# Moving the pair-maximum steps to other key-tile slots, and collecting the value products of long rows in groups of three, three and two

## The chip, the cores and the metric

One program runs on one core of a Trainium2 chip. The metric is the device time of one execution in microseconds (us): the median of three runs.

## The reference

Eight images of 1024 tokens and 256 channels pass through one block: a layer norm with a shift and a scale from a small modulation network, attention with 16 heads, a gated residual, a second layer norm, a mixture of 16 experts of which each token and head takes two, and a second gated residual. The part that the change touches is the attention:

```python
q = jnp.concatenate([q_content, q_rope], axis=-1)      # 16 + 32 columns a head
k = jnp.concatenate([k_content, k_rope], axis=-1)
scores = jnp.einsum('bhqd,bhkd->bhqk', q, k) * scale
scores = jnp.where(causal[None, None], scores, -jnp.inf)
attn = jax.nn.softmax(scores, axis=-1)
out = jnp.einsum('bhqk,bhkd->bhqd', attn, v)           # v: 16 columns a head
```

## The kernel before

The images follow one another. Each has an attention phase (about 161 us) and an expert phase (about 193 us) in which the next image's projections, and the first steps of its attention, are woven into the expert work. TensorE (PE in the profile), VectorE (DVE), ScalarE (ACT), GpSimd (POOL) and SyncE (SP, which only issues DMAs) each run one written order of instructions, and semaphores tie them.

**Slots.** The 16 heads make four groups `g`, the 1024 queries two halves `c`. A row is one (g, c), and `SEQ` orders the eight rows: (0,0), (1,0), (0,1), (2,0), (3,0), (1,1), (2,1), (3,1). A row of c = 0 has four key tiles of 128 keys, a row of c = 1 has eight, because the mask is causal. `MAIN` lists all 48 (g, c, key tile): they are the slots 0 to 47. Rows of eight key tiles take the slots 8 to 15, 24 to 31, 32 to 39 and 40 to 47. On the diagonal the moving side shrinks: the last four key tiles of a row have 512, 384, 256 and 128 query columns.

In a slot TensorE runs `scores` twice (L1279; one call is two heads of the group, four matmul instructions into two PSUM banks). ScalarE takes the exponential of each call from PSUM into a slot of the buffer `pt` (L1393), and GpSimd zeroes what the mask cuts (L1508). A call of `scores` may start when the exponential of the call before the last has freed its two banks. `values` (L1305) multiplies the exponentials of one key tile with the values: eight instructions for four heads. After every second slot the values of the last two key tiles are multiplied, so they stand at the end of the slots 2, 4, 6 and so on, and the last two in the first expert step. `pt` holds `PTS` = 6 calls, three key tiles, so the exponential of slot N waits for the values of slot N - 3.

**Pairs of maxima.** The exponentials need a bound of each query's scores. It comes from a second, cheaper multiplication in another number format: an item "pair" (L428) is two PSUM banks of such scores, and VectorE reduces each bank to a maximum (L573 where the mask cuts, L576 where it does not). An item stands in one of three parts of a slot: between the two calls of `scores`, behind the second, or in front of what follows. In the images after the first, 47 pairs are placed in the attention phase, and `PLACES` says where: (slot, part), part 0 being between and part 1 behind. In the first image other places are used (`per_slot`), two or three pairs in many slots.

**The ring.** Pairs and all other small items of the attention phase share a ring of three PSUM banks (6, 7, 5) in the order in which they are written down. A pair takes two of them. So a pair that follows another pair directly waits until VectorE has read the first bank of that one; if an item of one bank stands between the two, it waits for both banks. TensorE runs in order, so the calls of `scores` and the values behind a waiting pair wait with it. VectorE reads the items in the same order. When the last pair of a row is read, a `row` item (L500) turns the maxima, and SyncE moves them into the operand of the scores (L780, four DMAs) before the row begins.

Other items of the phase: `rope` (L477, L479), `sums` (L505: the row's outputs, turned), `tr` (L510), `o` (L518: the output projection, followed on VectorE by statistics), `xn` (L649 on VectorE: the second layer norm, four instructions), `tr2`, `tm`, `lg` and the choice of experts. At slot 22 VectorE multiplies three sets of weights by gates (L1474, L1476, L1478).

`L.va` holds the values: 32 columns a head, of which 16 are values, one is 1.0 (for the sum of the softmax) and 15 are 0.0. It lies in the region `front`; `pt` and, later, the expert buffers lie in the region `rest`.

Of the kernel before, what the change touches and what calls it, by code (L numbers as in the profile page):

```python
# [21 lines left out]
B, T, C = 8, 1024, 256  # L22
# [8 lines left out]
NP = NH // 2  # L31
MROW = QD
VW = 32
SCALE = float(QD) ** -0.5
NEG = -1e38
PTS = 6
FH, FD, NE, FI = 8, 32, 16, 128
XS = 3 * FD + 2
EPS_RMS, EPS_LN = 1e-6, 1e-5
# [145 lines left out]
        all_images(nc, L, Opening(nc, L))  # L185


FRONT_WORDS = 15248
HEADS_WORDS = 4096
WIDE_WORDS = 12288  # L190
REST_WORDS = 10496


class Regions:
# [25 lines left out]

    def place(self, L):
        self.begin("front")
        L.va = self.take("front", NT, NH, VW)
        base = self.at["front"]
        L.ht = self.take("front", CH, T)
        L.qct = self.take("front", T)
        L.ck = self.take("front", 2, T)
        L.rc = self.take("front", 2, T)
        L.rt = self.take("front", 3, 2, HALF)
        L.mx0 = self.take("front", NG, 4 * HG)  # L230
        L.mx1 = self.take("front", NG, 4 * HG, 2)
# [12 lines left out]
        gt0 = self.take("front", HALF)  # L244

        self.begin("heads")
        self.begin("wide")
        qk = [self.take("heads", 2, T) for _ in range(2)] + [self.take("wide", 2, T) for _ in range(6)]
        L.q2, L.k2 = qk[0::2], qk[1::2]
        self.begin("wide")  # L250
        L.x2 = self.take("wide", 2, FH, HALF)[0:XS].bitcast(F32R)
        L.gb = self.take("wide", 4, 2, HALF)

        self.begin("rest")
        L.wfg = self.take("rest", CH, C)
        L.bog = self.take("rest", C)
        own = self.at["rest"]
        L.wog = self.take("rest", CH, C)
        shared = self.at["rest"]
        L.pt = self.take("rest", PTS, 2, HALF)  # L260
        L.ot = self.take("rest", 2, HALF)
        self.begin("rest", REST_WORDS - 2 * HALF)
        L.junk_a = [self.take("rest", HALF) for _ in range(2)]

        self.begin("rest", shared)
        L.hm = self.take("rest", 4, T)
        L.ct = self.take("rest", CH, T)
        L.gy = self.take("rest", 3, HALF)
        L.kvt = self.take("rest", HALF)
        self.take("rest", HALF)  # L270
        part = self.take("rest", HALF)
        self.begin("rest", own)
        L.junk_b = [part, self.take("rest", HALF)]
        L.kvsq = L.junk_b[0]
        L.gt = [gt0, L.junk_b[0]]
        L.xn = L.ao
        L.cq = L.ao[:, :, :].rearrange("p t c -> p (t c)").rearrange("p (a t) -> p a t", a=2)
# [134 lines left out]
def item_matmuls(pe, L, R, item):  # L412
# [98 lines left out]
    elif kind == "o":  # L511
        c, n = item[1:]
        R.wait(pe, L, ("tr", c, CH - 1))
        if c == 0:
            pe.wait_ge(S["d0_w"], 5)
        for t in range(2):
            for k in range(CH):
                mm = pe.matmul(out[:, t * C:(t + 1) * C], L.at[:, k, (2 * n + t) * P:(2 * n + t + 1) * P], L.wog[:, k, :],  # L518
# [230 lines left out]
def front_ones(g, L):  # L749

    g.memset(L.va[:, :, :, HD:HD + 1], 1.0).then_inc(L.S["f_one"], 1)
    g.memset(L.va[:, :, :, HD + 1:VW], 0.0).then_inc(L.S["f_one"], 1)


def input_ones(sp, L, c):
# [141 lines left out]
class Opening:  # L897
# [4 lines left out]
    def __init__(self, nc, e):  # L902
# [5 lines left out]
        self.ct = e.lay.view("rest", 4352, CH, B)  # L908
        self.cs = e.lay.view("rest", 4368, CH, B)
        self.m01 = e.lay.view("rest", 5376, 2 * C)[0:B]  # L910
        self.m25 = e.lay.view("rest", 8448, 4, C)[0:B]
        self.g1 = e.lay.view("rest", 0, 2, C)[0:B]
        self.g2 = e.lay.view("rest", 768, 2, C)[0:B]
        self.wmod = e.wmod.rearrange("(k p) n -> p k n", p=P)
# [188 lines left out]

AHEAD = 2
EARLY = 3
PLACES = [(1, 0), (2, 0), (3, 0), (5, 0), (7, 0)]
PLACES += [(s, part) for s in range(9, 37) for part in range(2 - s % 2)]


def attend_slots(img):  # L1110
# [3 lines left out]
    if img:  # L1114
        slots[1][1].extend([("out", 2), ("out", 3)])
        places = PLACES
        pairs = [("pair", 1, *p) for p in PAIRS[1][AHEAD:AHEAD + 5]]
        pairs += [("pair", g, *p) for g in (2, 3) for p in PAIRS[0]]
        pairs += [("pair", 1, *p) for p in PAIRS[1][AHEAD + 5:]]
        pairs += [("pair", g, *p) for g in (2, 3) for p in PAIRS[1]]  # L1120
    else:
        per_slot = [(0, 2), (1, 2), (2, 3), (3, 2), (4, 3), (5, 3), (8, 2), (9, 1), (10, 2), (11, 2), (12, 3), (13, 1), (14, 2), (15, 1),
# [98 lines left out]
    return SEQ.index((g, c)) if j == 4 * c + 3 else None  # L1221


def unit(u):

    return u // (4 * NE), u // (2 * NE) % 2, u // 2 % NE, u % 2


def all_images(nc, L, O):
# [18 lines left out]
    with nc.Block() as block:  # L1248
        @block.tensor
        def _(pe):  # L1250
# [33 lines left out]
            def values(img, N):  # L1284
                g, c, j = MAIN[N]
                f = first_query(c, j)
                pe.wait_ge(S["c_exp"], 2 * (N + 1))
                if diag_upto[N]:
                    pe.wait_ge(S["c_sel"], diag_upto[N])
                if N == 0 and img:  # L1290

                    pe.wait_ge(S["e_gy"], NQ - 1)
                    RE[img - 1].wait(pe, L, ("v", 1))
                elif N == 0:

                    pe.wait_ge(S["f_one"], 2)
                    O.R.wait(pe, L, ("v", 1))
                    name, count = O.R.last(PVB)
                    pe.wait_ge(S[name], count)
                if j == 0 and SEQ.index((g, c)):  # L1300

                    pe.wait_ge(S["c_o"], SEQ.index((g, c)))
                for h in range(HG):
                    u = 2 * N + h // 2
                    mm = pe.matmul(bank(PVB)[h * VW:(h + 1) * VW, f:HALF], L.va[:, j, HG * g + h, :],  # L1305
                                   L.pt[:, u % PTS, h % 2, f:HALF], start=(j == 0), stop=(j == 4 * c + 3))
                mm.then_inc(S["c_pv"], 1)

# [36 lines left out]
            for img in range(B):  # L1345
                for s, (between, behind, front) in enumerate(aslots[img]):
# [10 lines left out]
                        outer(img - 1, NQ - 1)  # L1357
                    for item in behind + front:
                        item_matmuls(pe, L, RA[img], item)
                    if s and s % 2 == 0:  # L1360
                        values(img, s - 2)
                        values(img, s - 1)
                for q in range(NQ):
                    inner(2 * q)
                    inner(2 * q + 1)
                    if q == 0:
                        values(img, NM - 2)
                        values(img, NM - 1)
                    if q:
                        outer(img, q - 1)  # L1370
                    for item in eslots[img][q]:
# [6 lines left out]
        def _(act):  # L1378
            def weights(img, N, pr):
# [1 line left out]
                f = first_query(c, j)  # L1381
                u = 2 * N + pr
                act.wait_ge(S["c_s"], u + 1)
                if N >= 3:

                    act.wait_ge(S["c_pv"], N - 2)
                elif N == 2 and img:

                    act.wait_ge(S["c_rp"], RA[img].start["out", 3] + 1)
# [13 lines left out]
            def gelu(u):  # L1403
# [3 lines left out]
                    act.wait_ge(S["e_l2"], (u - HM) // 2 + 1)  # L1407
                else:

                    act.wait_ge(S["c_pv"], NM - 2 + u // 2)  # L1410
                nc.scalar.activation(L.hm[:, u % HM, :], bank(2 * (u % 2), 2), ACT.Gelu).then_inc(S["e_gelu"], 1)  # L1411

            O.scalar(act)
# [17 lines left out]
        def _(v):  # L1431
# [29 lines left out]
            for img in range(B):  # L1461
                for s, (between, behind, front) in enumerate(aslots[img]):
# [6 lines left out]
                    if s == 22:  # L1469
# [3 lines left out]
                        for k in range(CH):  # L1473
                            v.tensor_tensor(L.wog[:, k, :], L.wos[:, k, :], L.gate[:, 0, :],  # L1474
                                            ALU.mult).then_inc(S["d0_w"], 1)
                            v.tensor_tensor(L.wfg[:, k, :], L.wfs[:, k, :], L.gate[:, 1, :],  # L1476
                                            ALU.mult).then_inc(S["d0_w"], 1)
                        v.tensor_tensor(L.bog[:, :], L.bor[:, :], L.gate[:, 1, :], ALU.mult).then_inc(S["d0_w"], 1)  # L1478
# [214 lines left out]
```

## Time and profile before

| | us |
|---|---|
| Median of three runs | 2917.65 (2917.25 to 2918.07) |
| The profiled execution | 2920.5 |
| Its span, first to last instruction | 2918.1 |
| PE busy | 2816.6 (97%) |
| DVE busy | 1863.0 (64%) |
| ACT busy | 1808.5 (62%) |
| POOL busy | 1246.2 (43%) |
| PE L1279 (scores), two groups | 486.3 and 168.0 |
| PE L1305 (values) | 290.2 |
| PE L428 (pairs), two groups | 269.9 and 75.5 |

Starts and durations are in microseconds from the span's start. In a row of the timeline the two numbers are the start and the length of a run of like instructions, and a bracket tells for how long the engine stood idle before and what released it. Matmul instructions overlap, so a cost is best read from start to start.

### The profile page before, as it was taken

The page shows a single profiled execution, that of the slowest core. Times are in us where ns is not written, and L with a number is a line of the kernel's source. Part 1 is how long each engine was busy: PE and PEld are TensorE (multiplying, and loading weights), DVE is VectorE, ACT ScalarE, POOL GpSimd, SP SyncE. Part 2 cuts the span into 40 slices and gives each one's busy share as a digit, 9 for nine tenths or more (in the row PEclk, how much of TensorE's full clock was granted, in tenths as well). Part 3 has the DMA queues.
Part 4 walks back from the last instruction along what each step waited for, and adds up shares of the span by engine and source line. Part 5 has one row for each costly group of instructions (what it writes and reads, how often), then busy time and mean ns, then how long its engine had stood idle before and what let it go on. Part 6 is the DMA issues. An engine that isn't in the chain of part 4 may idle for free.

```text
span 2918.1 us, 50109 instructions
## 1 busy us (share of the span) xinstructions
PE 2816.6 (97%) x16476; PEld 1241.9 (43%) x16476; DVE 1863.0 (64%) x4638; ACT 1808.5 (62%) x2148; POOL 1246.2 (43%) x1325
## 2 busy tenths in 40 slices
PE   7899999999999999999999999999999999999999
PEld 3344444444444443444444444444444444444433
DVE  5775666756666666666667666675756657667553
ACT  2346675566755677457675576655666566665687
POOL 4312645136451364414654146531565215561254
PEclk9899999999999999999999999999999999999999
DMA  6203453044430444304432055311453124530343
GB/s 156 57 5 99 118 130 73 1 108 122 120 71 8 119 118 107 71 21 121 122 97 61 23 134 130 87 47 46 121 133 89 32 71 119 124 88 20 77 127 94
DMA packets 176972, 252.96 MB, mean 87 GB/s; under 512 B 50509, under 2 KB 83293, under 8 KB 176621
## 3 DMA queue, kind: packets, MB, share of 16 engines
q1 hardware_dynamic: 176100, 248.44, 34.3%
q8 instruction: 136, 2.23, 0.3%
q10 hardware_dynamic: 620, 1.34, 0.2%
q14 instruction: 116, 0.95, 0.1%
HBM read 159.13 MB, written 12.63 MB: 59 GB/s over the span
## 4 chain that ended last, share of the span: by engine, by line
PE 86%; DVE 7%; issue 3%; ACT 2%; POOL 1%; SPq 1%; DMA 1%; ACTq 0%; DVEq 0%; POOLq 0%
PE ps L1279 17%; PE ps L1321 17%; PE ps L1339 16%; PE ps L1305 9%; PE ps L428 7%; PE ps L477 4%; PE ps L479 2%; PE ps L518 2%; PE ps L548 2%; DVE rest L573 1%; PE ps L529 1%; PE ps L505 1%; PE ps L536 1%; PE ps L463 1%; PE ps L487 1%
## 5 line engine op out<-in xcount | busy, mean ns | idle before, releaser
L1411 ACT ACTIVATE rest<-ps 128x1024 f32<-128x1024 f32 x1024 | 993.8, 1024 | 341.1 <-PE ps L1321 340.9
L1393 ACT ACTIVATE rest<-ps 128x1024 f32<-128x1024 f32 (+3 forms) x768 | 610.2, 809 | 537.4 <-PE ps L1279 511.6
L1518 POOL TENSOR_TENSOR rest<-rest 128x512 f32<-128x512 f32 x478 | 632.0, 1322 | 560.7 <-DVE rest L1448 548.1
L1448 DVE SCALAR_TENSOR_TENSOR rest<-ps,b2c,wide 128x512 f32<-128x512 f32 x512 | 384.0, 750 | 489.8 <-PE ps L1339 451.7
L1321 PE MATMUL ps<-wide,w1s 98*128 98x512 f32 x2048 | 655.1, 437 | 11.5 <-ACT rest L1411 8.7
L1339 PE MATMUL ps<-rest,w2s 128*32 128x512 f32 x4096 | 546.1, 605 | 0.6 <-ACT rest L1411 0.6
L1508 POOL TENSOR_SCALAR_AFFINE_SELECT rest<-rest 128x256 f32<-128x256 f32 x512 | 206.4, 411 | 772.3 <-ACT rest L1393 770.3
L573 DVE CUSTOM_DVE_ANT_0 rest<-ps,maskd 128x512 f32<-128x512 f32 (+3 forms) x1024 | 444.8, 487 | 118.8 <-PE ps L428 114.0
L1279 PE MATMUL ps<-wide 49*128 49x512 f32 (+3 forms) x2304 | 486.3, 511 | 10.2 <-ACT rest L1393 4.2
L1321 PEld LDWEIGHTS ps<-wide,w1s 98*128 98x128 f32 x2048 | 340.8, 188 | 301.0 <-ACT rest L1411 189.0
L576 DVE TENSOR_REDUCE front<-ps 128x1 f32<-128x512 f32 x512 | 329.0, 684 | 92.9 <-PE ps L428 88.7
L428 PE MATMUL ps<-wide 48*128 48x512 f32 (+3 forms) x1152 | 269.9, 500 | 37.8 <-DVE front L573 20.7
L1305 PE MATMUL ps<-rest,front 128*32 128x512 f32 (+3 forms) x3072 | 290.2, 496 | 0.0
L1279 PEld LDWEIGHTS ps<-wide 49*128 49x128 f32 x2304 | 195.5, 186 | 195.7 <-issue 121.3
L726 POOL TENSOR_TENSOR front<-front,sin 128x512 f32<-128x512 f32 x128 | 163.7, 1279 | 110.5 <-DVE front L607 110.2
L428 PEld LDWEIGHTS ps<-wide 48*128 48x128 f32 x1152 | 108.0, 187 | 219.1 <-DVE front L573 79.1
L1279 PE MATMUL ps<-heads 49*128 49x512 f32 (+3 forms) x768 | 168.0, 520 | 2.8 <-DMA heads<-front 2.6
L739 POOL TENSOR_TENSOR front<-front 128x512 f32<-128x512 f32 x128 | 163.0, 1273 | 10.0
L1339 PEld LDWEIGHTS ps<-rest,w2s 128*32 128x32 f32 x4096 | 80.6, 108 | 191.0 <-issue 189.5
L1305 PEld LDWEIGHTS ps<-rest,front 128*32 128x32 f32 x3072 | 80.7, 110 | 163.0 <-issue 113.5
L477 PE MATMUL ps<-front,wkr 128*128 128x512 f32 x256 | 125.5, 619 | 0.0
L1279 PEld LDWEIGHTS ps<-heads 49*128 49x128 f32 x768 | 66.7, 191 | 66.0 <-issue 43.8
(142 smaller groups left out, 2192.4 us busy)
## 6 DMA issues: line engine op xcount, KB each, us to landing
wide<-gate_rows SPq DMA_DIRECT2D x1024, 128.0 KB, 2.8
wide<-front SPq DMA_DIRECT2D x480, 64.0 KB, 2.0
wide<-front SPq DMA_DIRECT2D x192, 128.0 KB, 2.3
ao<-in_x SPq DMA_DIRECT2D x16, 512.0 KB, 5.1
heads<-front SPq DMA_DIRECT2D x64, 128.0 KB, 2.3
xs<-in_x SPq DMA_DIRECT2D x16, 512.0 KB, 5.0
out<-xs SPq DMA_DIRECT2D x32, 256.0 KB, 2.7
wide<-ao SPq DMA_DIRECT2D x96, 64.0 KB, 2.3
```

The source lines that it names most:

```text
L428: mm = pe.matmul(outs[hh][:, at:at + w], L.q2[g][rows, pr, i * P:(i + 1) * P].bitcast(F32R), L.k2[g][rows, pr, keys].bitcast(F32R), start= ...
L477: mm = pe.matmul(out, L.wkr[:, k, hd], L.ht[:, k, half(c)], start=(k == 0), stop=(k == CH - 1))
L573: ins = v.tensor_tensor_reduce(out=R.junk[hh][:, at:at + w], in0=src[:, at:at + w], in1=L.maskd[:, HALF - w:], scale=1.0, scalar=-3e38, op ...
L576: ins = v.tensor_reduce(dst, src[:, 0:w], AX.X, ALU.max)
L1279: mm = pe.matmul(bank(2 * (u % 2) + hh)[:, 0:HALF - f], L.k2[g][rows, pr, j * P:(j + 1) * P], L.q2[g][rows, pr, c * HALF + f:(c + 1) * HAL ...
L1305: mm = pe.matmul(bank(PVB)[h * VW:(h + 1) * VW, f:HALF], L.va[:, j, HG * g + h, :], L.pt[:, u % PTS, h % 2, f:HALF], start=(j == 0), stop= ...
L1321: mm = pe.matmul(bank(2 * (u % 2) + k), L.w1s[:, e, :], L.x2[:, c, 4 * j + 2 * p + k, :], start=True, stop=True)
L1339: mm = pe.matmul(bank(L2 + q % 2)[FD * h:FD * h + FD, :], L.w2s[:, e, :], L.hm[:, (2 * q + h // 2) % HM, (h % 2) * HALF:(h % 2 + 1) * HALF ...
L1393: nc.scalar.activation(L.pt[:, u % PTS, :, f:HALF], L.ps[:, 2 * (u % 2):2 * (u % 2) + 2, 0:HALF - f], ACT.Exp, scale=SCALE).then_inc(S["c_ ...
L1411: nc.scalar.activation(L.hm[:, u % HM, :], bank(2 * (u % 2), 2), ACT.Gelu).then_inc(S["e_gelu"], 1)
L1448: v.scalar_tensor_tensor(out=dst, in0=bank(L2 + q % 2), scalar=L.b2c[:, e:e + 1], in1=L.gb[:, q // 2 % GB, q % 2, :], op0=ALU.add, op1=ALU ...
L1518: g.tensor_tensor(dst, dst, L.gy[:, k % GY, :], ALU.add).then_inc(S["e_add"], 1)
```

## The change

- `PLACES`, used in the images after the first, has another list. Before: one pair in the slots 1, 2, 3, 5 and 7, and from slot 9 to 36 two in even slots (between and behind) and one in odd slots (between). After: one in the slots 1, 2, 3, 4, 5, 7 and 8; from 9 to 36 one, except two in 10, 12, 25, 27, 29, 33 and 35, three in 26, 28 and 36 (two between and one behind) and none in 24. The order of the pairs changes so that seven of group 1 come first instead of five.
- The values of a row of eight key tiles are multiplied in groups of three, three and two, except in the last row, where they stay in twos like those of the short rows. In all images they then stand in the slots 2, 4, 6, 8, 11, 14, 16, 18, 20, 22, 24, 27, 30, 32, 35, 38, 40, 42, 44, 46.
- `pt` has 8 places instead of 6, and the waits of the exponentials and of the first expert activations follow from that.
- The values have 17 columns a head in place of 32. The matmul still takes 32 columns, which reach into the next head's, and gives PSUM rows that nothing reads. The memset of the 1920 columns of zeros becomes one of 16 columns.
- Of the five multiplications by the gates at slot 22, three move to slot 39.
- One opening buffer (`m25`) lies in another region.

```diff
-PTS = 6
+PTS = 8
-        L.va = self.take("front", NT, NH, VW)
+        L.va = self.take("front", NT, NH, VS)
+        L.va_end = self.take("front", VW // 2)
...
-            pe.wait_ge(S["d0_w"], 5)
+            pe.wait_ge(S["d0_w"], CH)
...
-PLACES = [(1, 0), (2, 0), (3, 0), (5, 0), (7, 0)]
-PLACES += [(s, part) for s in range(9, 37) for part in range(2 - s % 2)]
+SOON = 7
+SHARE = {10: 2, 12: 2, 24: 0, 25: 2, 26: 3, 27: 2, 28: 3, 29: 2, 33: 2, 35: 2, 36: 3}
+PLACES = [(s, 0) for s in (1, 2, 3, 4, 5, 7, 8)]
+PLACES += [(s, 2 * k // SHARE.get(s, 1)) for s in range(9, 37) for k in range(SHARE.get(s, 1))]
...
-        pairs = [("pair", 1, *p) for p in PAIRS[1][AHEAD:AHEAD + 5]]
+        pairs = [("pair", 1, *p) for p in PAIRS[1][AHEAD:AHEAD + SOON]]
...
+def value_groups():
+    groups, first = {}, 0
+    for g, c in SEQ:
+        for n in (2, 2, 2, 2) if (g, c) == SEQ[-1] else ((2, 2), (3, 3, 2))[c]:
+            groups[first + n] = range(first, first + n)
+            first += n
+    return groups
...
-                    if s and s % 2 == 0:
-                        values(img, s - 2)
-                        values(img, s - 1)
+                    for N in GROUPS.get(s, ()):
+                        values(img, N)
...
-                if N >= 3:
-                    act.wait_ge(S["c_pv"], N - 2)
+                if N >= 4:
+                    act.wait_ge(S["c_pv"], N - 3)
+                elif N == 3 and img:
+                    act.wait_ge(S["e_add"], 15 * NQ // NE)
...
                             v.tensor_tensor(L.wog[:, k, :], L.wos[:, k, :], L.gate[:, 0, :],
                                             ALU.mult).then_inc(S["d0_w"], 1)
+                    if s == 39:
+                        for k in range(CH):
                             v.tensor_tensor(L.wfg[:, k, :], L.wfs[:, k, :], L.gate[:, 1, :],
```

## Rows read from the trace of the kernel before

**Rows 1.** Waits of PE: who, for whom, us in total, times, longest
```profile
PE ps L428 <- DVE front L573: 21.5, 41, 1.0
PE ps L428 <- DVE front L576: 12.3, 22, 3.0
```

**Rows 2.** Windows, third image, slots 8-15, 16-23, 24-31, 32-39: length, busy by engine
```profile
838.18:864.50 26.32, 25.42 (x171) 10.63 (x170) 16.43 (x70) 13.98 (x17) 8.11 (x12) 1.00 0.34 91
864.50:886.48 21.98, 20.88 (x167) 10.75 (x167) 18.45 (x53) 12.45 (x19) 6.54 (x17) 1.00 0.01 3
886.48:913.03 26.55, 25.57 (x172) 10.91 (x172) 17.63 (x49) 15.41 (x20) 3.50 (x9) 1.00 0.00 1
913.03:945.09 32.06, 31.01 (x184) 14.37 (x184) 19.55 (x56) 15.74 (x20) 4.96 (x11) 1.00 0.02 5
```

**Rows 3.** Timeline of PE, third image, slot 26: scores, pair, scores, pair, values
```profile
893.34 1.13 PE L1279 MATMUL ps<-wide 49*128 49x512 f32 x4
893.90 0.80 PE L428 MATMUL ps<-wide 48*128 48x512 f32 x2
894.54 1.02 PE L1279 MATMUL ps<-wide 49*128 49x512 f32 x4
895.58 0.51 PE L428 MATMUL ps<-wide 48*128 48x512 f32 x2
896.01 1.92 PE L1305 MATMUL ps<-rest,front 128*32 128x512 f32 x16
```

**Rows 4.** Timeline of PE, third image, slots 42 to 44, which hold no pair
```profile
952.23 1.99 PE L1279 MATMUL ps<-wide 49*128 49x512 f32 x8
954.14 1.92 PE L1305 MATMUL ps<-rest,front 128*32 128x512 f32 x16
...
955.03 1.04 PE L1305 MATMUL ps<-rest,front 128*32 128x512 f32 x8
956.00 1.99 PE L1279 MATMUL ps<-wide 49*128 49x512 f32 x8
958.25 2.04 PE L1279 MATMUL ps<-wide 49*128 49x512 f32 x8 [0.26 <-ACT rest L1393]
```

**Rows 5.** Timeline of PE, third image, slot 14 (256 columns): its pair behind
```profile
861.37 0.49 PE L428 MATMUL ps<-wide 48*128 48x512 f32 x2 [0.50 <-DVE front L573]
```

**Rows 6.** Timeline of DVE, third image: a pair read (L576), and xn (L649)
```profile
894.74 1.29 DVE L576 TENSOR_REDUCE front<-ps 128x1 f32<-128x512 f32 x2 [0.57 <-PE ps L428]
...
927.81 1.37 DVE L649 TENSOR_SCALAR front<-xs,tmv,tstd 128x256 f32<-128x256 f32 x4
```

**Rows 7.** Timeline of PE, first image, slots 35 and 36: pair, scores, pair
```profile
219.26 0.50 PE L428 MATMUL ps<-wide 48*128 48x512 f32 x2
219.57 1.05 PE L1279 MATMUL ps<-wide 49*128 49x512 f32 x4
220.61 0.50 PE L428 MATMUL ps<-wide 48*128 48x512 f32 x2
```

**Rows 8.** Timeline of PE, first image, slot 12: two pairs between the scores
```profile
132.58 1.13 PE L1279 MATMUL ps<-heads 49*128 49x512 f32 x4
...
134.90 0.49 PE L428 MATMUL ps<-wide 48*128 48x512 f32 x2 [0.95 <-DVE front L573]
135.21 1.04 PE L1279 MATMUL ps<-heads 49*128 49x512 f32 x4
```

**Rows 9.** Timeline of PE, first image, rope of slot 11, first scores of 16 and 18
```profile
130.66 1.98 PE L477 MATMUL ps<-front,wkr 128*128 128x512 f32 x4
...
148.50 2.08 PE L1279 MATMUL ps<-wide 49*128 49x512 f32 x4 [2.78 <-DMA wide<-front]
...
158.50 0.70 PE L1279 MATMUL ps<-wide 49*128 49x256 f32 x4
```

**Rows 10.** Windows, first image: length, busy by engine; granted clock third from right
```profile
144.00:147.00 3.00, 1.72 (x24) 0.89 (x16) 2.13 (x12) 0.77 (x2) 0.77 (x2) 1.00 1.01 293
...
149.00:151.00 2.00, 2.00 (x8) 0.88 (x7) 0.00 (x0) 0.37 (x1) 0.00 (x0) 0.50 0.00 0
```

More of the change, by code:

```diff
@@ L33 @@
 VW = 32
+VS = HD + 1
 SCALE = float(QD) ** -0.5
 NEG = -1e38
-PTS = 6
+PTS = 8
 FH, FD, NE, FI = 8, 32, 16, 128
@@ L185, in build @@
         all_images(nc, L, Opening(nc, L))
-FRONT_WORDS = 15248
+FRONT_WORDS = 14176
 HEADS_WORDS = 4096
 WIDE_WORDS = 12288
-REST_WORDS = 10496
+REST_WORDS = 11520
 class Regions:
@@ L222, in place @@
         self.begin("front")
-        L.va = self.take("front", NT, NH, VW)
+        L.va = self.take("front", NT, NH, VS)
+        L.va_end = self.take("front", VW // 2)
+        L.va_all = self.view("front", 0, NT * NH * VS + VW // 2)
         base = self.at["front"]
@@ L261, in place @@
         L.ot = self.take("rest", 2, HALF)
-        self.begin("rest", REST_WORDS - 2 * HALF)
         L.junk_a = [self.take("rest", HALF) for _ in range(2)]
@@ L751, in front_ones @@
     g.memset(L.va[:, :, :, HD:HD + 1], 1.0).then_inc(L.S["f_one"], 1)
-    g.memset(L.va[:, :, :, HD + 1:VW], 0.0).then_inc(L.S["f_one"], 1)
+    g.memset(L.va_end, 0.0).then_inc(L.S["f_one"], 1)
 def input_ones(sp, L, c):
@@ L910, in __init__ @@
         self.m01 = e.lay.view("rest", 5376, 2 * C)[0:B]
-        self.m25 = e.lay.view("rest", 8448, 4, C)[0:B]
+        self.m25 = e.lay.view("front", FRONT_WORDS - 4 * C, 4, C)[0:B]
         self.g1 = e.lay.view("rest", 0, 2, C)[0:B]
@@ L1116, in attend_slots @@
         places = PLACES
-        pairs = [("pair", 1, *p) for p in PAIRS[1][AHEAD:AHEAD + 5]]
+        pairs = [("pair", 1, *p) for p in PAIRS[1][AHEAD:AHEAD + SOON]]
         pairs += [("pair", g, *p) for g in (2, 3) for p in PAIRS[0]]
-        pairs += [("pair", 1, *p) for p in PAIRS[1][AHEAD + 5:]]
+        pairs += [("pair", 1, *p) for p in PAIRS[1][AHEAD + SOON:]]
         pairs += [("pair", g, *p) for g in (2, 3) for p in PAIRS[1]]
@@ L1221, in sums_done @@
     return SEQ.index((g, c)) if j == 4 * c + 3 else None
+def value_groups():
[5 more added lines that the diff above has]
+    return groups
+GROUPS = value_groups()
 def unit(u):
@@ L1304, in values @@
                     u = 2 * N + h // 2
-                    mm = pe.matmul(bank(PVB)[h * VW:(h + 1) * VW, f:HALF], L.va[:, j, HG * g + h, :],
+                    mm = pe.matmul(bank(PVB)[h * VW:(h + 1) * VW, f:HALF], L.va_all[:, VS * (NH * j + HG * g + h):VS * (NH * j + HG * g + h) + VW],
                                    L.pt[:, u % PTS, h % 2, f:HALF], start=(j == 0), stop=(j == 4 * c + 3))
@@ L1366, in _ @@
                     if q == 0:
-                        values(img, NM - 2)
-                        values(img, NM - 1)
+                        for N in GROUPS[NM]:
+                            values(img, N)
                     if q:
@@ L1408, in gelu @@
                 else:
[L1410 removed]
+                    act.wait_ge(S["c_pv"], NM - 3 + u // 2)
                 nc.scalar.activation(L.hm[:, u % HM, :], bank(2 * (u % 2), 2), ACT.Gelu).then_inc(S["e_gelu"], 1)
```

## The prediction

> **What bounds the kernel now.** I read the page's busy shares first: TensorE is busy 97% of the span, so only work or waits on TensorE can move the time. Then the waits of TensorE [rows 1]: those before a pair, on VectorE's reading of an earlier pair, lead the list, though in one execution they come to only 34 us; the view misses waits that hide in overlapping instructions. So I took the PE timeline of one image, start to start, and the windows over its long stretches [rows 2]. The second to the eighth image repeat one pattern, and slots 8 to 39 of one take 26.32 + 21.98 + 26.55 + 32.06 = 106.91 us. VectorE has 17 to 20 busy in stretches of 22 to 32: not full on average, but full wherever pairs follow closely.
>
> **Unit prices.** Two full calls of scores take 1.92, full values of two key tiles 1.86 [rows 4]. In slot 26 the second scores start at 1.20 and its pair at 2.24, values at 2.67: a pair between costs 1.20 - 0.96 = 0.24, one behind, ahead of values, 2.67 - 2.16 = 0.51 (2.16 = 1.20 + 0.96) [rows 3]. Behind and ahead of scores it costs 0.39: 0.31 in place of 0.43 [rows 7]. These are prices without a wait. The wait rule is the ring: a pair may start when VectorE has read the first bank of the last. VectorE starts 0.84 after a pair that is between (893.90 to 894.74), holds 1.29 for both banks, some 1.4 where the mask splits them, and the next pair goes 0.84 after VectorE's start, half a read and a hand-over of 0.15 to 0.2 [rows 3, 6]. So pairs stand at least 1.35 apart (219.26 to 220.61) [rows 7]. Two pairs between the scores are seen in the first image: its slot 12 has them, and the scores that should start 1.20 into the slot start at 135.21 - 132.58 = 2.63 [rows 8]. The second pair costs 1.43, against 0.24.
>
> **Part by part, an image of the last seven.** Removed pairs and stalls first. Slots 16 to 23 lose their four pairs behind: 4 x 0.51, and two of these slots, 256 columns wide, also held waits as that of slot 14 [rows 5]: 4 x 0.51 + 2 x 0.50 = -3.0. In slots 8 to 15, slot 14 loses a pair behind and most of its wait: -1.03; slot 8 gains a pair between, +0.24; slots 11 and 13 now follow a pair with no values to hide its reading, +0.15 and +0.43; the cheaper "behind" of 10 and 12 gives -0.25. Sum -0.46. Slot 4: +0.24.
>
> Slots 24 to 31 take fourteen pairs where twelve stood, and thirteen of them fall in slots 25 to 30. Slot 24 loses two and a wait behind the five gate multiplications: -1.42. I then walked the ring, each pair at the later of its own place and the reading it waits for. Slot 25: its second pair and the `sums` item behind it, +0.69. Slot 26: the first pair waits until both banks of slot 25's are read (VectorE has `sums` to read besides), so VectorE starts 1.53 into the slot; the next pair goes 0.84 later, 2.37; scores at 2.68; third pair at 3.80, slot end at 4.11. Before it was 2.67 without values: +1.45. Slot 27: second pair, +0.84. Slot 28, two between again with `tr` behind: +1.46. Slot 29: +0.99. Slot 30 loses a pair but waits for both banks of slot 29's: only -0.55. Sum +3.46.
>
> Slots 32 to 39: slot 32 loses a pair, -0.50. Slot 33 gains one, +0.69. Slot 34 loses one and a wait on VectorE's work for `o`, -1.31. Slot 35 gains one behind, and in VectorE's order `xn` (1.37) now lies ahead of both pairs of the slot [rows 6]: 0.42 for the pair, 1.18 for the wait, +1.60. Slot 36, two between: +1.25, and slot 37 starts too early for ScalarE, +0.20. Sum +1.93.
>
> Values in threes: three fewer groups. A second key tile starts 0.89 after the first and ends the group after 0.97 (954.14, 955.03, 956.00) [rows 4], so a dropped end saves 0.09: -0.27. Bounds 0 to 0.15 each. Without values between them, scores are paced by ScalarE: 2.25 a slot (956.00 to 958.25) in place of 1.92 [rows 4], but a slot with a pair has 2.16 anyway; I count 0.1 in slot 34 and take the 3-slot runs as covered by their pairs. If that cover is gone, it costs 0.1 a slot.
>
> Total: -3.0 - 0.46 + 0.24 + 3.46 + 1.93 - 0.27 = +1.9 us an image, +13.3 for seven. Put otherwise, ten pairs move: taking them out frees 1.03 + 3.0 + 1.42 + 0.55 + 0.50 + 1.31 = 7.8, putting them in costs 9.45, 0.95 each, and the rest is +0.26.
>
> **The first image** keeps its pairs; only values move. Slot 10 no longer ends with 1.86 of values, so the last rope of slot 11 (130.66) runs 1.86 earlier. A chain of SyncE's DMAs hangs on it (rope, its moves, the modulation rows, loads, then the row's maxima), and slot 16 waits for its end, 2.78 us [rows 9]. So slot 16 starts 1.86 sooner, and the wait shrinks to some 0.7 us. After the wait the granted clock falls to 0.50, which is 1.2 GHz, in the window from 149; before it was 1.00 with TensorE busy about half [rows 10]. A wait of 1.0 elsewhere in the attention leaves no such fall [rows 1]; I take it as avoided: slots 16 and 17 take 10.0 now (148.50 to 158.50) [rows 9] and 7.5 by the unit prices, -2.5 (bounds -2.5 and 0). Slots 24 to 36 lose cover as above, `xn` above all: +0.8. Sum -3.6.
>
> The page "TensorE: Matmul & The Clock Gate" of the Trainium skill (Part 1) says an idle array falls back to half clock and sustained work releases it; the trace agrees with the fall. By that rule any wait left there could still trigger it, and the sum would be 2.5 higher.
>
> **At nothing.** Three gate multiplications in slot 39 (1.3 us of VectorE): it is idle there between the `tlo` steps and before `lg`; if not, up to 1.3 an image. The short memset: GpSimd idles behind it in the opening. Weight loads of 32 columns at a stride of 17: they hide under the four-tile matmuls; bounds 0 and, if each of eight per key tile showed 10 ns, +0.08 a key tile, 4 an image; I take 0, since it stays 32 contiguous columns. More places in `pt`: no exponential waits for values now. Extra waits (slot 3's on the expert sums) are met several us before. The row maxima of slots 17 and 21 reach slots 20 and 24 some 0.2 us before they are needed, by my walk: close, and up to +0.5 each if late.
>
> **Sum.** 13.3 - 3.6 = +9.7. The span of 2918.1 becomes 2927.8 (the profiled execution lies 2.4 beyond its span, and that stays); on the median of 2917.65 it is 2927.3.
>
> **Rivals.**
> A, faster: VectorE keeps up. The added pairs then cost 0.24 to 0.51 without waits, 10 x 0.45 = 4.5 in place of 9.45, while the removed 7.8 are real: +1.9 - 4.95 = -3.05 an image, -21.4 - 3.6, about 2893. For it: VectorE is idle a third of these stretches [rows 2]. Against: the one double-between I can see paid 1.43 [rows 8]. It decides at 0.81 an added pair: there the seven images lose 3.6, which is what the first gains.
> B, about the same: waits half of what my walk gives, because a delayed scores call later spares a wait on ScalarE. Added pairs at 0.75: -0.1 an image, -0.7 - 3.6 = 2913.3, and 2911 to 2921 with the prices between.
> C, slower still: the backlog runs through the ring, the row maxima come late and delay slots 20, 24 and 32. +1 an image more: 2935 to 2945.
> D, only the groups matter: 8 x 3 x 0.09 = 2.2 us less, 2915.5. The page "TensorEngine Tiling (Array Packing)" of the Trainium skill (Key Properties) says that changing the tiling mode drains the array, which speaks for fewer groups. The row's price is the 0.09 above; an exit that cost the whole 0.15 would give 3.6.
>
> **How the numbers follow.** Forecast (2921 to 2935) 0.52; A 0.14; B and D 0.24; C 0.10. About 0.2% (5.8 us) is what a measurement of this kernel can tell from no change. Slower by more (over 2923.5): most of the forecast's cases and C, 0.58. Faster by more (under 2911.8): A and a few of B, 0.18. Same: 0.24. Range 2908 to 2938: it leaves out A, and the far half of C.
>
> **What would show it.** In the PE timeline: slots 16 to 23 at 18.9 or 19.0 in place of 21.98; slots 24 to 31 near 29.9 and 32 to 39 near 33.9; the second pair between in slots 26, 28 and 36 starting 2.2 to 2.4 into its slot, with a bracket on VectorE; in slot 35 the pair behind waiting 1.2 for VectorE with L649 ahead; the first image's slot 16 starting 1.9 us earlier with no window at 0.50. Wrong, if those three second pairs start under 1.5 into the slot (then A), or if the slots 9 to 15 also lose.

## The result and the profile after

The changed kernel takes 2925.58 us (median, 2922.64 to 2930.65) beside 2918.06 of the kernel before on the same chip (2917.25 to 2919.18): a ratio of 1.0025, with a 95% interval of 1.0016 to 1.0035. It is slower by 7.5 us, where +9.7 was forecast. Its profiled execution took 2926.29, with a span of 2923.9, which is 5.8 above the span of before.

The windows over the third image's slots 8-15, 16-23, 24-31 and 32-39, after (columns as in [rows 2]: length, then busy time of PE, PEld, DVE, ACT and POOL, then the granted clock of TensorE):

```profile
839.21:865.00 25.79, 25.08 (x171) 10.64 (x170) 16.42 (x70) 14.11 (x17) 8.13 (x12) 1.00 0.38 93
865.00:883.93 18.93, 18.75 (x156) 9.74 (x157) 13.01 (x34) 12.16 (x19) 6.53 (x17) 1.00 0.01 3
883.93:913.62 29.69, 27.02 (x176) 11.45 (x176) 19.77 (x61) 15.42 (x20) 3.25 (x9) 1.00 0.00 1
913.62:947.28 33.66, 31.51 (x187) 14.68 (x187) 21.69 (x61) 15.80 (x20) 4.96 (x11) 1.00 0.04 8
```

Slots 16 to 23 lose 3.04 us and are 99% busy now. Slots 24 to 31 are 3.14 longer, and TensorE is idle there for 2.67 of 29.69. The waits of PE in the whole span (who waits for whom, us in total, times, longest), after, against [rows 1]:

```profile
PE ps L430 <- DVE front L575: 26.3, 35, 1.1
PE ps L430 <- DVE front L578: 18.9, 30, 2.8
PE ps L1296 <- DMA wide<-front: 2.7, 5, 1.4
```

The two waits of a pair on VectorE's reading grew from 33.8 to 45.2 us. The third line is the row's maxima: their DMA was late before some scores, for 1.42 us in the first image (2.78 before) and four times, 1.24 together, in the others. (L430 is L428 of before, L575 and L578 are L573 and L576, L1296 is the scores, L1322 the values, L651 is `xn`.)

The forecast named three second pairs. Here are slots 26, 28 and 36 of the third image in PE's timeline (start, us, operation, idle before it and who ended it):

```profile
889.97 1.13 PE L1296 MATMUL ps<-wide 49*128 49x512 f32 x4
891.04 0.50 PE L430 MATMUL ps<-wide 48*128 48x512 f32 x2
892.39 0.51 PE L430 MATMUL ps<-wide 48*128 48x256 f32 x4 [0.84 <-DVE front L578]
892.70 1.06 PE L1296 MATMUL ps<-wide 49*128 49x512 f32 x4
...
900.33 1.13 PE L1296 MATMUL ps<-wide 49*128 49x512 f32 x4
900.89 0.80 PE L430 MATMUL ps<-wide 48*128 48x512 f32 x2
902.57 0.50 PE L430 MATMUL ps<-wide 48*128 48x512 f32 x2 [0.88 <-DVE front L575]
...
932.40 1.13 PE L1296 MATMUL ps<-wide 49*128 49x512 f32 x4
932.96 0.80 PE L430 MATMUL ps<-wide 48*128 48x512 f32 x2
934.64 0.50 PE L430 MATMUL ps<-wide 48*128 48x512 f32 x2 [0.88 <-DVE front L575]
```

They start 2.42, 2.24 and 2.24 into their slots, each with 0.84 or 0.88 us of TensorE's idle time ahead and VectorE as the releaser: 2.2 to 2.4 was forecast, under 1.5 would have been rival A.

The pair behind in slot 35, first PE and then DVE:

```profile
927.08 1.04 PE L1296 MATMUL ps<-wide 49*128 49x512 f32 x4
929.26 0.50 PE L430 MATMUL ps<-wide 48*128 48x512 f32 x2 [1.14 <-DVE front L575]
```

```profile
925.94 1.28 DVE L578 TENSOR_REDUCE front<-ps 128x1 f32<-128x512 f32 x2
927.13 1.37 DVE L651 TENSOR_SCALAR front<-xs,tmv,tstd 128x256 f32<-128x256 f32 x4
928.42 0.68 DVE L575 CUSTOM_DVE_ANT_0 rest<-ps,maskd 128x512 f32<-128x512 f32 x1
```

`xn` runs first (1.37), then the first bank of the slot's first pair is read, and only when that is done does the second pair go. It waits 1.14; 1.2 was forecast.

Slot by slot, start to start, third image, worked out from the scores' starts in both timelines (slots not listed differ by 0.01 or less; where values move to another slot, only a run of slots that holds as many of them before as after can be compared):

```
slots      4     8    9-14   16    18    20    21    22    24    25   26-30   32    33   34-38
before   4.62  4.62  20.63  3.43  3.89  3.42  2.65  3.93  4.12  2.74  18.61  5.42  4.51  19.56
after    4.86  4.86  19.86  2.94  2.94  2.94  2.51  2.95  2.71  3.33  22.59  4.92  5.10  21.09
```

The opening and the first image together bring 0.26 us in the profiled execution: 257.63 us to the first expert phase before, 257.37 after.

### The profile page after: what moved, and what is told of

Same layout as the page of the kernel before. It is cut to its first block, busy times and chain, and to the rows that moved or that the text cites. A ratio compares the mean times of both kernels' runs of the same rounds, so it can differ in the third digit from the quotient of the medians.

```text
span 2923.9 us, 50107 instructions
## 1 busy us (share of the span) xinstructions
PE 2807.9 (96%) x16476; PEld 1238.9 (42%) x16476; DVE 1861.7 (64%) x4638; ACT 1808.7 (62%) x2148; POOL 1243.7 (43%) x1325
## 4 chain that ended last, share of the span: by engine, by line
PE 84%; DVE 7%; issue 4%; ACT 2%; POOL 1%; DMA 1%; SPq 1%; ACTq 0%; DVEq 0%; POOLq 0%
PE ps L1296 17%; PE ps L1338 17%; PE ps L1356 15%; PE ps L1322 9%; PE ps L430 7%; PE ps L479 4%; PE ps L481 2%; PE ps L550 2%; PE ps L520 2%; PE ps L531 1%; DVE front L578 1%; PE ps L538 1%; PE ps L465 1%; PE ps L507 1%; DVE rest L1467 1%
## 5 line engine op out<-in xcount | busy, mean ns | idle before, releaser
L575 DVE CUSTOM_DVE_ANT_0 rest<-ps,maskd 128x512 f32<-128x512 f32 (+3 forms) x1024 | 444.6, 486 | 151.3 <-PE ps L430 146.7
L1296 PE MATMUL ps<-wide 49*128 49x512 f32 (+3 forms) x2304 | 485.9, 508 | 9.9 <-ACT rest L1412 4.2
L578 DVE TENSOR_REDUCE front<-ps 128x1 f32<-128x512 f32 x512 | 328.7, 683 | 102.5 <-PE ps L430 98.5
L430 PE MATMUL ps<-wide 48*128 48x512 f32 (+3 forms) x1152 | 263.0, 488 | 53.2 <-DVE front L575 25.4
L1322 PE MATMUL ps<-rest,front 128*32 128x512 f32 (+3 forms) x3072 | 284.7, 494 | 0.0
L1296 PEld LDWEIGHTS ps<-wide 49*128 49x128 f32 x2304 | 197.8, 186 | 174.8 <-issue 100.1
L430 PEld LDWEIGHTS ps<-wide 48*128 48x128 f32 x1152 | 109.0, 188 | 251.4 <-DVE front L575 91.0
L1296 PE MATMUL ps<-heads 49*128 49x512 f32 (+3 forms) x768 | 169.2, 518 | 2.8 <-DMA heads<-front 2.8
L1322 PEld LDWEIGHTS ps<-rest,front 128*32 128x32 f32 x3072 | 82.9, 109 | 188.9 <-issue 137.5
L609 DVE STREAM_SHUFFLE front<-ps 128x512 f32<-128x512 f32 x128 | 94.3, 737 | 0.0
```

Of the source, the lines that this page charges most:

```text
L430: mm = pe.matmul(outs[hh][:, at:at + w], L.q2[g][rows, pr, i * P:(i + 1) * P].bitcast(F32R), L.k2[g][rows, pr, keys].bitcast(F32R), start= ...
L575: ins = v.tensor_tensor_reduce(out=R.junk[hh][:, at:at + w], in0=src[:, at:at + w], in1=L.maskd[:, HALF - w:], scale=1.0, scalar=-3e38, op ...
L578: ins = v.tensor_reduce(dst, src[:, 0:w], AX.X, ALU.max)
L1296: mm = pe.matmul(bank(2 * (u % 2) + hh)[:, 0:HALF - f], L.k2[g][rows, pr, j * P:(j + 1) * P], L.q2[g][rows, pr, c * HALF + f:(c + 1) * HAL ...
L1322: mm = pe.matmul(bank(PVB)[h * VW:(h + 1) * VW, f:HALF], L.va_all[:, VS * (NH * j + HG * g + h):VS * (NH * j + HG * g + h) + VW], L.pt[:, ...
```

## Experiments

All compare with the kernel before on the same chip. "An image" is one of the last seven; its numbers are those of the third image, unless said.

**1. The places alone.** The kernel before, with only the new list:

```
-PLACES = [(1, 0), (2, 0), (3, 0), (5, 0), (7, 0)]
-PLACES += [(s, part) for s in range(9, 37) for part in range(2 - s % 2)]
+SOON = 7
+SHARE = {10: 2, 12: 2, 24: 0, 25: 2, 26: 3, 27: 2, 28: 3, 29: 2, 33: 2, 35: 2, 36: 3}
+PLACES = [(s, 0) for s in (1, 2, 3, 4, 5, 7, 8)]
+PLACES += [(s, 2 * k // SHARE.get(s, 1)) for s in range(9, 37) for k in range(SHARE.get(s, 1))]
...
```

> The kernel before with the new places of the pairs alone: values stay in twos, the buffer and the layout stay. Theory R (the ring: a pair waits until VectorE has read the pair ahead): slots 16 to 23 fall from 21.98 to about 18.9, slots 24 to 31 grow from 26.55 to 29.3 to 30, slots 32 to 39 from 32.06 to 33.3 to 33.9, each later image costs 1.2 to 1.9 us more, and as the first image keeps its order the total is +8 to +13, 2926 to 2931. Rival G (the loss comes from the long runs of scores without values, paced by ScalarE, and the new places alone are a gain): slots 24 to 39 stay within 0.5 of before and the total falls by 3 us an image or more, under 2898.

Measured: 2928.51, ratio 1.0038 (1.0025 to 1.0051). Slots 4-7 +0.24, 8-15 -0.61, 16-23 -3.04, 24-31 +3.09, 32-39 +0.48. So the loss of slots 24 to 31 is there without the new groups. The 32-39 term missed: 33.3 to 33.9 us was expected, 32.54 came. In its slot 34 the values still stand in twos, and `xn` runs under them:

```profile
928.68 1.37 DVE L649 TENSOR_SCALAR front<-xs,tmv,tstd 128x256 f32<-128x256 f32 x4
930.59 0.69 DVE L573 CUSTOM_DVE_ANT_0 rest<-ps,maskd 128x512 f32<-128x512 f32 x1 [0.53 <-PE ps L428]
```

VectorE is idle for 0.53 between them, waiting for TensorE, and the next pair behind (931.44) starts with no bracket. So the places alone cost +0.16 in the third image, 1.1 if all seven were alike. The time rose by 10 nevertheless, and the profiled span by 8.2. In three of the seven images slots 24-31 took 4.7 more, not 3.1, which is 4.9 together, and there the granted clock fell. Another 2.9 lie in slots 8-23 of five images, 0.2 to 0.9 each: the row's maxima come late there, and the scores of slots 16 and 20 wait for their DMA ten times in the seven images, up to 1.11 us. So the total of 2926 to 2931 came out as expected by luck: an image lost 0.16 by the ring, not 1.2 to 1.9, and most of the rest was clock and late maxima. In the second image:

```profile
535.39 0.50 PE L428 MATMUL ps<-wide 48*128 48x512 f32 x2
536.73 0.50 PE L428 MATMUL ps<-wide 48*128 48x256 f32 x4 [0.83 <-DVE front L576]
```

```profile
536.00:541.00 5.00, 4.20 (x22) 1.37 (x26) 3.90 (x12) 1.53 (x2) 0.00 (x0) 0.77 0.00 0
538.80:542.10 3.30, 3.30 (x18) 0.45 (x10) 1.16 (x2) 0.35 (x1) 0.00 (x0) 0.50 0.00 0
```

Behind the wait, TensorE has work in every one of 3.30 us, at a clock of 0.50, which is 1.2 GHz.

**2. All but the places**: the changed kernel with the old places. The groups, the layout, `pt` and the moved gate products stay:

```
-SOON = 7
-SHARE = {10: 2, 12: 2, 24: 0, ...}
-PLACES = [(s, 0) for s in (1, 2, 3, 4, 5, 7, 8)]
+SOON = 5
+PLACES = [(1, 0), (2, 0), (3, 0), (5, 0), (7, 0)]
+PLACES += [(s, part) for s in range(9, 37) for part in range(2 - s % 2)]
...
```

> The changed kernel with the old places of the pairs: only the groups of values, the buffer of eight places, the layout and the moved gate products are left. Theory R: groups save 0.27 an image and uncover the reading behind slots 10, 12, 26, 28 and 34 for 0.1 to 0.4 each, so a later image changes by 0 to +0.7; the first image's slot 16 starts earlier and loses its half-clock windows (up to -4); total 2914 to 2921. Rival G: a later image costs 1.2 us or more, total 2926 or more.

Measured: 2911.38, ratio 0.9978 (0.9969 to 0.9987). Slots 8-15 +0.23, 24-31 -0.53, 32-39 -0.13. Without the places the other parts are faster than before, so the slowdown comes with the places. Both expectations, 0 to +0.7 an image and 2914 to 2921, were too high: the gain in slot 24, which experiment 3 sets apart, is not among their terms. In the first image slot 16 waits 0.84 in place of 2.78 [rows 9]; slot 15, which holds that wait, falls from 3.73 to 1.79, and slots 16-23 lose 2.56, where 2.5 was forecast (other runs of these instructions do not repeat that; see the first image below):

```profile
145.91 1.13 PE L1295 MATMUL ps<-wide 49*128 49x512 f32 x4 [0.84 <-DMA wide<-front]
```

**3. The layout alone**, as experiment 2, but with values in twos:

```
-        for n in (2, 2, 2, 2) if (g, c) == SEQ[-1] else ((2, 2), (3, 3, 2))[c]:
+        for n in ((2, 2), (2, 2, 2, 2))[c]:
```

> The changed kernel with the old places and with values in twos everywhere: only the buffer of eight places, the 17 columns a head, and the gate products in slot 39 are left. Theory R: slot 24 loses part of its wait on VectorE (0.3 to 0.7 an image), nothing else in the attention moves; the expert phase, 0.2 shorter in the changed kernel, is 0.2 shorter here too if the layout makes it; total 2912 to 2917. A rival that the loads of 17-column values cost time: slots with values grow by 0.05 or more each, total over 2925.

Measured: 2912.64, ratio 0.9981 (0.9972 to 0.9991), not to be told from experiment 2. In the attention of an image only slot 24 changes, 4.12 to 3.50. The pair between in that slot had waited on VectorE, which was at gate multiplications ahead of its reading of slot 23's pair: it started 2.29 us after that pair, and starts 1.36 after it now, which is about the smallest distance, 1.35 [rows 7]. Three of the five multiplications now lie in slot 39, and nothing is longer there. Weight loads at a stride of 17 columns and the longer `pt` cost nothing that shows in any slot. The shorter memset lies in the opening, where half clock comes and goes and the profiles differ by up to 2.8 us; nothing can be told of it.

**4. Pairs behind the values**, the other way to give VectorE time. The kernel before, where the second pair of even slots 10 to 36 of the later images goes last in its slot, after the values:

```
-PLACES += [(s, part) for s in range(9, 37) for part in range(2 - s % 2)]
+PLACES += [(s, part) for s in range(9, 37) for part in ((0,) if s % 2 else (0, 3))]
...
                         values(img, s - 1)
+                    for item in last:
+                        item_matmuls(pe, L, RA[img], item)
```

> The kernel before with the second pair of every even slot 10 to 36 moved from ahead of the values to behind them, in images after the first. Theory R: a pair then stands at least 1.9 us from the one ahead, so the waits of slots 14, 18, 22, 30 and 34 (0.5 to 1.0 each) go, a pair ahead of scores costs 0.39 in place of 0.51, and new waits of 0.1 (512 columns), 0.3 (384) and 0.7 (128) come in the odd slots behind: -2 to -4 us an image, total 2890 to 2905. Rival G (pairs and VectorE do not set the time): within 3 us of before.

Measured: 2938.45, ratio 1.0069 (1.0048 to 1.0090). A clear miss: 2890 to 2905 was expected. The pair is now far from its predecessor and near its successor. Slot 14 falls from 4.36 to 3.68 but slot 15 rises from 1.07 to 1.57, slot 18 from 3.89 to 3.28 and slot 19 from 1.07 to 1.56. Slot 24 grows from 4.12 to 6.48:

```profile
884.72 0.50 PE L428 MATMUL ps<-wide 48*128 48x512 f32 x2 [0.74 <-DVE front L573]
885.03 1.28 PE L1279 MATMUL ps<-wide 49*128 49x128 f32 x8
887.90 0.51 PE L428 MATMUL ps<-wide 48*128 48x256 f32 x4 [1.59 <-DVE front L576]
888.21 1.56 PE L1279 MATMUL ps<-wide 49*128 49x512 f32 x4
```

```profile
886.00:888.00 2.00, 0.41 (x4) 0.13 (x3) 2.00 (x5) 1.02 (x1) 0.54 (x1) 1.00 0.00 0
890.00:892.00 2.00, 2.00 (x20) 1.17 (x14) 0.04 (x1) 1.41 (x2) 0.00 (x0) 0.50 0.00 0
```

TensorE is busy for 0.41 of the 2.00 us to 888.00 while VectorE is busy for all of it: until 887.07 at the five gate multiplications, which stand ahead of its reading of slot 23's pair, and slot 24's pair waits for that reading. From 888.6 the granted clock is 0.50. Five of the seven later images show such a stretch. The other two are 0.8 and 1.0 us longer than before, so the miss is not the clock's alone. A stall that is only moved is paid again, and here the longer one was followed by half clock besides.

**5. `xn` out of the way**, the changed kernel with `xn` queued behind slot 35's pairs:

```
-    slots[34][1].append(("xn", 0))
+    slots[35][2].append(("xn", 0))
```

> The changed kernel with the second layer norm's step xn (VectorE, 1.37 us) moved from slot 34 to the end of slot 35, behind that slot's two pairs, in every image. Theory R: the second pair of slot 35 no longer waits for it, slot 35 falls from 6.52 to about 5.35, slot 36 stays at 3.90 because the values hide the step: -1.2 us an image. Rival G (scores paced by ScalarE set slot 35): slot 35 stays within 0.3 of 6.52.

Measured in one run: 2918.29. Slot 35 falls from 6.52 to 5.39 in every later image; 5.35 was expected. Its pair behind has no bracket now:

```profile
922.98 1.04 PE L1296 MATMUL ps<-wide 49*128 49x512 f32 x4
924.02 0.50 PE L430 MATMUL ps<-wide 48*128 48x512 f32 x2
```

Slots 32-39 are at +0.47 against before, which is what the places alone gave. So 1.13 of the +1.60 there is `xn` having lost the values that hid it. The seven images together are 4.6 us shorter than in the profile of the changed kernel, where 8.4 was expected: in two of them, the third among them, the granted clock falls to 0.50 in slot 30, behind waits that the changed kernel has too, and slots 24-31 take 1.6 and 1.7 more.

**6. One pair back.** The changed kernel with one pair of slot 26 back in slot 24:

```
-SHARE = {10: 2, 12: 2, 24: 0, 25: 2, 26: 3, 27: 2, 28: 3, ...}
+SHARE = {10: 2, 12: 2, 25: 2, 26: 2, 27: 2, 28: 3, ...}
```

> The changed kernel with one pair less in slot 26 (two in place of three, so one between in place of two) and one more in slot 24, in images after the first. Theory R: slot 24 grows by 0.24 (2.71 to 2.95), slot 26 falls from 4.17 to 2.7 or 2.8, the second pair between having cost 1.35 to 1.45; -1.2 us an image. Rival K (VectorE's total work in the stretch sets it, not the place): slots 24 to 31 together fall by less than 0.4.

Measured in one run: 2921.27. Slot 24 goes from 2.71 to 2.95 (the 0.24 of a pair between), slot 25 from 3.33 to 3.55, slot 26 from 4.17 to 2.63: -1.07 for the stretch, with -1.2 expected, and -7.1 for the seven images. Rival K gave less than 0.4. The pair too many in slot 26 cost about a whole turn of the ring (1.54 there, 0.22 of it paid again in slot 25), not the 0.24 to 0.51 of its own work. Slot 26 now:

```profile
889.18 1.13 PE L1296 MATMUL ps<-wide 49*128 49x512 f32 x4
889.93 0.62 PE L430 MATMUL ps<-wide 48*128 48x256 f32 x4
890.38 1.03 PE L1296 MATMUL ps<-wide 49*128 49x512 f32 x4
891.50 0.50 PE L430 MATMUL ps<-wide 48*128 48x512 f32 x2
```

**7. Pairs spread as evenly as they go.** The layout of experiment 3, values in twos, a pair in each of slots 1 to 36 and a second one in eleven slots that have time for it:

```
-SOON = 5
+SOON = 11
...
+TWICE = (2, 4, 8, 10, 12, 16, 20, 26, 28, 32, 36)
+PLACES = [(s, part) for s in range(1, 37) for part in range(2 if s in TWICE else 1)]
```

> The kernel with the new layout, the moved gate products and values in twos, and a third set of places by the prices of theory R: all eleven pairs left of group 1 in slots 1 to 8 (second ones in 2, 4 and 8 behind a rope), one between in every slot from 9 to 36, a second one only behind full-width scores ahead of values (10, 12, 16, 20, 26, 28, 32, 36). Theory R: slots 0 to 8 grow by about 2.2, slots 14, 18, 22, 24, 30 and 34 fall by 1.42, 0.95, 0.99, 1.1, 1.30 and 1.41: -5 us an image, total 2878 to 2890. Rival K (VectorE's total work sets the time): the sum over an image changes by less than 1 us, total over 2905.

Measured: 2899.39, ratio 0.9942 (0.9926 to 0.9959), faster than both kernels, though 2878 to 2890 was expected. An image is 2.9 shorter, where 5 was expected: slots 14, 18, 22, 24, 30 and 34 lose 1.0, 0.9, 1.0, 1.2, 1.0 and 1.4, while slots 0-8 grow by 3.0. The expectation had 2.2 for slots 0-8 and 1.3 to 1.4 each for slots 14 and 30. Slots 2, 4 and 8 grow by 0.52, 0.67 and 0.66, about the prices of their pairs. Slot 6 grows by 0.92, not by the 0.24 of a pair between. Its pair starts 1.12 into the slot, against 0.35 in slot 2, and waits for VectorE, which is at a `rope` item (L610) whose bank the pair needs:

```profile
827.88 0.50 PE L430 MATMUL ps<-wide 48*128 48x512 f32 x2 [0.42 <-DVE front L610]
```

The waits of PE:

```profile
PE ps L430 <- DVE front L578: 7.0, 8, 3.0
PE ps L1295 <- DMA wide<-front: 6.3, 9, 2.8
PE ps L430 <- DVE front L575: 5.0, 13, 1.0
```

Pairs wait 12.0 us for VectorE in place of 33.8 [rows 1]. The second line was 2.8 before, all of it in the first image: the row's maxima are now late in every later image too, by 0.2 to 0.9 before slot 16, and three of the images lose some 0.4 to 0.6 more in slots 8-15 by it.

**8. The same, with slot 36's second pair in slot 37**, the last row's maxima a slot later, and the first image's values in threes (for the earlier slot 16 of experiment 2):

```
-TWICE = (2, 4, 8, 10, 12, 16, 20, 26, 28, 32, 36)
-PLACES = [(s, part) for s in range(1, 37) for part in range(2 if s in TWICE else 1)]
+TWICE = (2, 4, 8, 10, 12, 16, 20, 26, 28, 32)
+PLACES = [(s, part) for s in range(1, 38) for part in range(2 if s in TWICE else 1)]
...
+        slots[37][1].append(("rmax", 3))
+        slots[38][0].append(("row", 3, 1))
```

> The spread kernel with two more edits: the first image alone takes its values in threes, and in the later images the second pair of slot 36 stands between the scores of slot 37, with the row maxima of the last row turned in slot 38. Theory R: the first image's slots 15 and 16 together fall from 8.6 to about 5.3 (shorter wait on the DMAs, no half clock behind it) and its slots 32 to 39 give back 1.0; in later images slot 36 falls by about 0.5, slot 37 grows by 0.24, -0.3 an image; 3 to 5 us under the spread kernel, 2894 to 2897. Rival: the row maxima now come late for slot 40, which then grows by 0.3 or more in every image, and the total does not fall.

Measured: 2897.67, ratio 0.9925 (0.9908 to 0.9941), not to be told from experiment 7. Slot 36 falls by 0.50, slots 37 and 38 rise by 0.13 and 0.29: -0.09 an image with -0.3 expected. What the pair saved went to slots 37 and 38. Slot 40 stays at 4.63, so the rival falls. The first image missed: slots 15 and 16 take 7.78 together, where about 5.3 was expected. The wait on the DMAs is shorter, 1.40 in place of 2.79, but half clock follows it all the same (149.4 to 156.3), and slots 32-39 are 1.03 longer with the values in threes, where a gain of 1.0 was expected.

## Why the prediction was right, step by step

In us, the forecast with the merges put where they fall, and the third image:

```
slots           4-7    8-15   16-23   24-31   32-39   an image
forecast      +0.24   -0.55   -3.00   +3.37   +1.84     +1.9
measured      +0.24   -0.53   -3.04   +3.14   +1.60     +1.41
places alone  +0.24   -0.61   -3.04   +3.09   +0.48     +0.16
all but them  -0.01   +0.23   -0.02   -0.53   -0.13     -0.46
```

**The spacing of pairs was the right mechanism.** The 1.35 between pairs of [rows 7] is the 1.35 from 891.04 to 892.39 in slot 26 after. The walk of the ring gave slot 24 -1.42 (measured -1.41), slots 26 to 30 +4.10 (+3.98), slot 36 3.90 (3.90). Rival A falls by the three second pairs and by experiment 6. The full price of 1.43 for a second pair between [rows 8] carried the forecast, and the idle third of VectorE misled: where pairs follow closely, it is the distance from the last one that counts. Rival B falls for these slots by the same three rows: their waits are whole. One sign was ill put: the prediction called itself wrong "if the slots 9 to 15 also lose". They lose 0.77, but its own terms give -0.79 there, so this tells nothing against it.

**Terms that were too dear.** The second pairs of slots 25 and 33 cost 0.59, with 0.69 forecast; slots 26-30 and 34-38 came 0.12 each below the forecast. Seven images came to +10.67 (the sum over all seven, one of them 0.5 above the rest) against +13.3. The difference, 2.6, is in the terms' sizes and not in their signs.

**Places and groups are not additive, and the text treated them as nearly so.** The forecast gave `xn` 1.18 in slot 35 as part of the places' +1.60. The size was right (1.13 and 1.14 by experiment 5 and the bracket), the assignment was not: with values in twos the same places cost 0.48 in that stretch, with threes 1.60. The term should have stood with the groups. They took away the 1.86 of values that stood over VectorE's work. The first image, whose places did not change, shows the same: slots 32-39 are 1.04 longer in experiment 2 and unchanged in experiment 1. In the third image places cost 0.16 an image in the old groups and 1.41 + 0.46 = 1.87 in the new.

**Merged groups.** Forecast -0.27 an image for three dropped group ends. Experiment 2 less experiment 3 is -0.46 + 0.61 = +0.15: whatever the ends save, +0.23 in slots 8-15 takes back. The text had put lost cover there at 0.1 a slot only if it came. Rival D (only the groups matter, 2915.5) is false of the change, and of its parts too: experiment 2 came to 2911.38, but experiment 3, with no group merged, to 2912.64, so the gain is the moved gate products' in slot 24 (0.62 an image) and not the merges'. The rule that a change of the tiling mode drains the array ("TensorEngine Tiling (Array Packing)" of the Trainium skill, Key Properties) is neither borne out nor refuted by these runs; the ends are too small a part of what moved.

**The gates.** "At nothing" in slot 39 held. What they do in slot 24 is in the layout: -0.62 an image with the old places. With the new ones it adds nothing: slot 24 takes 2.70 in experiment 1, where the gates stay, and 2.71 after. The forecast's -1.42 counted it once, rightly, as a gain of the places.

**Row maxima.** Their margin of 0.2 us was as thin as said: four late ones in the later images, 0.18 to 0.63 us, and one image with +0.52 in slots 16-23. Rival C (every image +1) did not occur in the changed kernel. Late maxima do occur, though: the same places with values in twos had ten (experiment 1).

**The first image was wrong in its sum.** Forecast -3.6, measured -0.26 for all that lies ahead of the first expert phase. In this profile what was forecast is there: slot 16 waits less and no clock falls behind it (after):

```profile
149.67 1.13 PE L1296 MATMUL ps<-wide 49*128 49x512 f32 x4 [1.42 <-DMA wide<-front]
...
151.00:153.00 2.00, 1.99 (x24) 0.70 (x20) 1.90 (x5) 1.90 (x2) 0.41 (x1) 1.00 0.00 0
```

The wait is 1.42 in place of 2.78 (0.7 was forecast; slot 15 falls by 1.36, not 1.86), the clock stays at 1.00, and slots 16-23 lose 2.56. But slots 8-15 are 1.63 longer just ahead (the opening is 2.4 shorter, slots 0 to 7 are 1.9 longer), where half clock stands over ten microseconds after, and over 3.4 before (one window each, after and then before):

```profile
112.50:122.70 10.20, 9.98 (x34) 3.87 (x35) 4.72 (x15) 2.63 (x3) 2.54 (x2) 0.50 0.11 25
...
112.50:122.70 10.20, 9.30 (x46) 3.93 (x48) 7.40 (x22) 3.20 (x4) 3.83 (x3) 0.83 0.17 39
```

Nothing shows this to be the change's doing. Experiments 5 and 6 run the changed kernel's own instructions up to slot 23 of the first image, and there slots 0 to 15 took 83.21 and 85.42, against 90.01 in its profile and 86.47 before.

Nor is it shown that the change takes away the half clock behind slot 16. The shorter wait is the change's: it is 0.84 to 1.76 us in the five profiles with values in threes in the first image, and 2.55 to 2.79 in the five with twos. But half clock follows it in all five with twos and in three of the five with threes. One is experiment 6, with a wait of 1.68 and the same instructions as the changed kernel:

```profile
146.10:152.90 6.80, 6.80 (x32) 2.95 (x34) 2.62 (x8) 2.63 (x3) 0.82 (x2) 0.50 0.01 2
```

There slots 16-23 are 0.39 longer than before; in experiment 5 they are 1.19 shorter, and in the changed kernel 2.56. So two steps failed: "I take it as avoided", worth 2.5, which this profile met by chance, and the belief that one execution's stretches of half clock in the first image stay where they are when the work ahead shifts. Slots 32-39's +1.05 (from +0.8) came as forecast.

**The expert phases** (194.4 us each before), for which the forecast had no term, are 0.2 shorter in each of seven images, and the last one 3.2. The last is clock: before shows half clock at 2803 and 2909, after doesn't, and each experiment has at least one such stretch. The 0.2 are not explained: they come in small steps of 0.02 to 0.03, appear also in experiments 3 and 8, and not in experiments 5 and 6, which run the changed kernel's expert phase. So the change is not shown to make them.

Summed: 10.7 - 0.3 - 1.4 - 3.2 = 5.8, the difference of the spans. The medians differ by 7.5, because the profiled execution of before lay 2.4 above its median, and that of after 0.7 above. That 7.5 is so near to 9.7 is in part luck: the seven images came 2.6 below the forecast and the expert phases gave 4.6 that it did not have, while the first image came 3.3 above it, and the profiled executions stand for 1.7. The sign and most of the size are the ring's.

## What to carry to other kernels

Work that needs a bank, and another engine to empty it, has a smallest distance. List the starts, take the distance from one pair with a bracket, and walk the list: this gave each stretch of the changed kernel within 0.25 us, while busy shares pointed the other way. It gave the two kernels of experiments 4 and 7 less well: one came out slower where a gain was expected, and the other with three fifths of its gain an image. When such work is moved, look at both neighbours, and at what lies in the reading engine's queue; a matmul run that is merged away may have been the cover of a step that no one listed. Trying each part of a change alone pays even when the sum is forecast well: here the slow part hid a gain of 6 us in the others, and pairs spread by the same prices were worth about 12 more, 18 together with the layout.

## What the runs showed of the hardware that was not expected

A wait of 0.8 us ahead of full work can end in a stretch at 1.2 GHz (experiment 1, second image) or not (the same waits in its third image): slots 24-31 then take 31.3 or 29.6. Experiment 5 has the changed kernel's own instructions there, and falls in two of its seven later images, where the profile of the changed kernel falls in none. Experiment 4 has the longer wait, 1.59, with TensorE busy 0.41 of 2.00 us, and falls in five of seven. The prediction looked for such falls in the first image only, and took from its profile that a wait of 1.0 elsewhere leaves none; these runs show that it can. The page "TensorE: Matmul & The Clock Gate" of the Trainium skill (Part 1) has idle time as the cause; the rows agree in that waits stand ahead of each of these falls. Here they were short ones, and no run tells why the clock fell behind some and not behind others.

The places make more such waits, and the times lie further apart: 2923.5 to 2934.2 in five executions with the places alone, beside 2915.7 to 2923.6 in twenty of before on that chip; 2922.6 to 2930.7 in the changed kernel, beside 2917.3 to 2919.2. But experiment 7, with few such waits, has 2896.6 to 2904.4. That the falls make the scatter was not shown, since only the profiled executions tell the clock.
